# A rebuilt opening for a routed two-layer kernel: dense slots, four gathers at once, a joint first norm

## The reference

```
x = x + tanh(g_xattn) * xattn(layernorm(x), token_ids, ctx)
x = x + tanh(g_ffn)   * ffn(layernorm(x))
```

## Time and profile before

| | us |
|---|---|
| median of three runs | 538.0 (536.31 to 539.51) |
| the profiled execution | 538.59 |
| its span, first to last instruction | 536.8 |
| TensorE matmul busy | 465.1 (87%) |
| VectorE busy | 351.8 (66%) |
| ScalarE busy | 253.8 (47%) |
| GpSimd busy | 242.3 (45%) |
| mean granted clock of TensorE | 0.974 of full speed |

### The profile page before, as it was taken

One profiled execution on the slowest core, in us unless ns is written; L12 is line 12 of the kernel. 1 busy time (PEld: TensorE's weight loads), 2 busy tenths in 40 slices (PEclk: granted clock), 3 DMA queues, 4 the chain that ended last, 5 costly groups with the idle time before them and its releaser, 6 DMA issues.

```text
span 536.8 us, 9049 instructions
## 1 busy us (share of the span) xinstructions
PE 465.1 (87%) x2774; PEld 403.7 (75%) x2775; DVE 351.8 (66%) x766; ACT 253.8 (47%) x381; POOL 242.3 (45%) x266
## 2 busy tenths in 40 slices
PE   1058999999993699999998999999999999999970
PEld 1035777777882488778887999999999998988960
DVE  6657999999986643689485676666665555555510
ACT  4323444444543444621243666666665556555520
POOL 0545455555532000021463546566666656663542
PEclk9999999999998599999999999999999999999995
DMA  8407343444541644022473798888888889876553
GB/s 283 141 20 274 109 154 122 156 157 154 173 135 57 195 140 194 0 79 80 156 249 124 224 321 244 247 254 239 240 234 232 217 234 253 241 246 159 101 65 49
DMA packets 28665, 93.32 MB, mean 174 GB/s; under 512 B 4448, under 2 KB 4448, under 8 KB 28128
## 3 DMA queue, kind: packets, MB, share of 16 engines
q1 hardware_dynamic: 15696, 57.87, 32.9%
q0 software_dynamic: 12944, 35.14, 25.7%
HBM read 71.49 MB, written 23.07 MB: 176 GB/s over the span
## 4 chain that ended last, share of the span: by engine, by line
PE 31%; DMA 29%; DVE 14%; issue 10%; POOL 9%; ACT 3%; POOLq 1%; SPq 0%; DVEq 0%
DMA out<-ys,cur 24%; PE psG L995 17%; PE psY L995 11%; POOL out L424 5%; POOL cur L346 4%; PE psT L1000 3%; DMA front<-in_x,cur 2%; DMA raw<-in_ctx_t 2%; DVE nwt L767 1%; DMA xh<-xh_sb,cur 1%; DVE stats L737 1%; DVE nwt L775 1%; DVE nwt L768 1%; DVE slot L791 1%; DVE gu L717 1%
## 5 line engine op out<-in xcount | busy, mean ns | idle before, releaser
L995 PE MATMUL psY<-arena 128*128 (+1 forms) x372 | 91.6, 397 | 3.2 <-DVE arena L728 3.2
L346 POOL COPY cur<-idx 128x1 int32 (+1 forms) x121 | 50.3, 416 | 93.9 <-DMA out<-ys,cur 30.9
L995 PE MATMUL psG<-bl,slot 128*128 128x256 f32 (+1 forms) x648 | 89.1, 298 | 2.1 <-DVE bl L946 2.1
L995 PEld LDWEIGHTS psG<-bl,slot 128*128 128x128 f32 x648 | 84.1, 193 | 6.8 <-DVE bl L946 2.5
L995 PEld LDWEIGHTS psY<-arena 128*128 128x128 f32 x372 | 67.9, 188 | 17.1 <-issue 3.9
L424 POOL DMA_INDIRECT out<-ys,cur x32 | 64.8, 2025 | 26.6 <-POOL cur L346 18.2
L791 DVE TENSOR_TENSOR slot<-raw,slot 128x1536 fp32r<-128x1536 f32 x27 | 48.4, 1802 | 38.5 <-ACT slot L488 28.5
L995 PEld LDWEIGHTS psG<-bl,arena 128*128 128x128 f32 x576 | 70.0, 192 | 2.2 <-DVE bl L946 1.3
L995 PE MATMUL psG<-bl,arena 128*128 128x256 f32 x576 | 70.6, 283 | 0.9 <-DVE bl L946 0.9
L403 POOL TENSOR_TENSOR xh_sb<-ys,xb 128x512 f32<-128x512 f32 x16 | 21.4, 1339 | 94.8 <-ACT ys L529 84.9
L415 POOL DMA_INDIRECT ht<-xh,cur x32 | 51.0, 1595 | 25.5 <-POOL cur L346 16.5
(11 more groups left out here) (169 smaller groups left out, 621.9 us busy)
## 6 DMA issues: line engine op xcount, KB each, us to landing
raw<-in_w SPq DMA_DIRECT2D x51, 768.0 KB
ht<-xh SPq DMA_DIRECT2D x16, 256.0 KB, 2.8
xb<-xh SPq DMA_DIRECT2D x16, 256.0 KB, 3.0
out<-xh_sb SPq DMA_DIRECT2D x16, 256.0 KB, 2.0
raw<-in_ctx_t SPq DMA_DIRECT2D x2, 1024.0 KB, 8.1
ht<-in_ctx_t SPq DMA_DIRECT2D x1, 1024.0 KB, 11.1
xh_sb<-in_ctx_t SPq DMA_DIRECT2D x1, 1024.0 KB, 13.9
out<-log_sb SPq DMA_DIRECT2D x2, 256.0 KB, 12.9
```

Of the source, the lines that this page charges most:

```text
L346: pool.tensor_copy(cur[:, n:n + 1], table[:, bass.ds(q, 1), col]).then_inc(done, 1)
L995: ins = pe.matmul(ps, left[a], right[b], start=n == 0 and m == 0, stop=n == total - 1 and m == 2)
```

## The change

It touches the opening and the first layer's use of GpSimd. Nothing of the second layer is changed.

- Slots are dense: tokens sorted by expert get positions 0 to 2047 without padding, and slot p of tile `(position >> 7) + expert` is row `position & 127`. A tile in which two experts meet becomes two tiles with the same rows divided between them; there are 19 as before. The rounding of counts goes, a third small matmul (a lower triangle) and some additions come.
- The one-hot matrix is made from 2-byte operands (`digits`, which ScalarE copies from the constants, and `lo_digit`) and lies in `big_all` instead of `front`.
- VectorE makes all four low parts of the context: 0, 1 and 2 behind the index table, 3 at the end of step -1.
- The constants are loaded in two pieces; the loads of the ids and gates are issued by ScalarE.
- GpSimd sends the gathers of tiles 0 to 3 at once (2 and 3 into `ys`, which the first layer doesn't use), without `cur`: each indirect DMA names its column of `idx1`. Its steps are all unrolled.
- Tiles 1 and 2 are normed together in step -1; step 0 has no norm.

```diff
+            def rows_of(t, col):
+                return bass.IndirectOffsetOnAxis(ap=idx1[:, t, col:col + 1], axis=0)
+            def gather_xa(t):
+                if 4 <= t < 6:
+                    pool.wait_ge(h_ready, t - 3)
+                elif t >= 6:
+                    pool.wait_ge(h_ready, t - 1)
+                buf = ys[:, t % 2, :] if t in (2, 3) else xa[:, t % 2, :]
+                pool.indirect_dma_start(buf, None, x, rows_of(t, 0)).then_inc(xa_here[t if t < 4 else t % 2], 16)
+            def gather_xb(t):
+                if t >= 2:
+                    pool.wait_ge(x1_ready, t - 1)
+                pool.indirect_dma_start(xb[:, t % 2, :], None, x, rows_of(t, 0)).then_inc(xb_here[t % 2], 16)
...
+            for t in range(4):
+                gather_xa(t)
+            gather_xb(0)
+            gather_xb(1)
+            gather_xa(4)
+            gather_xa(5)
+            for t in range(2, LAST):
+                if t < NT:
+                    gather_xb(t)
+                if t + 4 < NT:
+                    gather_xa(t + 4)
+                scatter(t - 2)
```

On VectorE, the index table (`S` and `SI` are columns of scratch):

```diff
+            link(dve.tensor_tensor(S(3), S(1), S(2), ALU.add))
+            link(dve.tensor_tensor(S(3), S(3), S(7), ALU.add))
             dve.wait_ge(in_const, 16)
-            link(dve.tensor_tensor_scan(S(8, E1), cst[:, C_KEEP:C_KEEP + E1 * NJ], S(4, E1), 0.0, ALU.mult, ALU.add))
+            link(dve.tensor_tensor_scan(run, ones[:, 0:E1 * NJ], S(4, E1), 0.0, ALU.mult, ALU.add))
...
             dve.wait_ge(r1_pre, 1)
-            link(dve.tensor_scalar(cnt_i[:, 0, :], psY[0][:, E1:2 * E1], float(P - 1), None, ALU.add))
-            link(dve.tensor_scalar(cnt_i[:, 1, :], cnt_i[:, 0, :], -P, None, ALU.bitwise_and))
-            link(dve.tensor_copy(S(13)[:, 0:E1], cnt_i[:, 1, :]))
-            link(dve.tensor_tensor_scan(S(14)[:, 0:E1], ones[:, 0:E1], S(13)[:, 0:E1], 0.0, ALU.mult, ALU.add))
-            link(dve.tensor_tensor(S(15)[:, 0:E1], S(14)[:, 0:E1], S(13)[:, 0:E1], ALU.subtract))
-            link(dve.tensor_tensor(S(16)[:, 0:E1], S(15)[:, 0:E1], psY[0][:, 0:E1], ALU.add))
...
-            link(dve.tensor_copy(S(26, 2), SI(1, 2)))
-            dve.tensor_tensor(onehot[0], along(iota, NJ), over(S(26), P), ALU.is_equal)
+            dve.tensor_tensor(onehot1, along(digits[:, :], NJ), over(lo_digit[:, :], P), ALU.is_equal)
...
-            low_ctx(0)
             dve.wait_ge(r1_src, 1)
...
+            low_ctx(0)
             low_ctx(1)
+            low_ctx(2)
```

On VectorE, the step; `pair` is step -1, and its last Newton operation raises `norm_ready` by 2:

```diff
-                one, two = have(known, 2), have(known, -2)
+                one, two = have(known, 2) and known != 0, have(known, -2)
...
+                pair = known == FIRST + 1
+                cs = slice(0 if one else 1, 2 if two or pair else 1)
...
+                if pair:
+                    xa_landed(dve, 0, 0, 0)
+                    i = dve.bn_stats(stats[:, 1, :], xa_of(0, 0, 0))
...
+                        if pair and m == 0:
+                            low_h()
...
+                if pair:
+                    low_ctx(3)
```

On TensorE:

```diff
-            pe.matmul(psY[0][:, 0:E1], tri, S12(small)[:, 0:E1], start=True, stop=True)
+            pe.matmul(psY[0][:, 0:E1], tri, S12(small)[:, 1:E1 + 1], start=True, stop=False)
+            pe.matmul(psY[0][:, 0:E1], low_tri, S12(small)[:, 0:E1], start=False, stop=True)
```

More of the change, by code:

```diff
@@ L47 @@
 PAD = TOK
-C_ID, C_TRI, C_ONE, C_IOTA = 0, P, 2 * P, 3 * P
+C_TRI, C_LOW, C_ONE, C_IOTA = 0, P, 2 * P, 3 * P
 C_TOKP, C_TOKJ = 4 * P, 4 * P + NJ
-C_KEEP = C_TOKJ + NJ
+C_ID = C_TOKJ + NJ
+C_KEEP = C_ID + P
 C_EM = C_KEEP + E2 * NJ
@@ L194, in gated_layer @@
         xa_idx, xb_idx, xh_idx = sem("xa_idx"), sem("xb_idx"), sem("xh_idx")
-        xa_here = [sem(f"xa_here{n}") for n in range(2)]
+        xa_here = [sem(f"xa_here{n}") for n in range(4)]
         xb_here = [sem(f"xb_here{n}") for n in range(2)]
@@ L237, in gated_layer, with xa_of, xa_landed @@
         FIRST, LOOP0, LOOP1, LAST = -2, 5, 17, NT + 2
+        def xa_of(t, par, known):
+            return ys[:, par, :] if known in (0, 1) else xa[:, par, :]
+        def xa_landed(eng, t, par, known):
+            if known is not None and known < 2:
+                eng.wait_ge(xa_here[known + 2], 16)
+            else:
+                eng.wait_ge(xa_here[par], landed(t, par))
         def stage1(eng, step):
@@ L349, in index @@
                 return bass.IndirectOffsetOnAxis(ap=cur[:, n:n + 1], axis=0)
-            pool.wait_ge(r1_idx, 1)
[L352 to L364, removed]
@@ L479, in step @@
                         act.wait_ge(hT_ps, t + 1)
-                    norm(h[:, par, :], xa[:, par, :], 0, h_ready)
+                    norm(h[:, par, :], xa_of(t, par, known), 1 if known == 0 else 0, h_ready)
                 if have(known, -2):
@@ L738, in step @@
                 k = t + 2
-                if not (one or two):
-                    dve.tensor_copy(stats[:, 0, 0:1], cst[:, 0:1]).then_inc(norm_ready, 1)
-                else:
+                if one or two:
                     i.then_inc(stats_done, 1)
@@ L748, in step @@
                         i = dve.bn_aggr(mv[:, 0, :], stats[:, 0, :])
-                    if two:
+                    if two or pair:
                         i = dve.bn_aggr(mv[:, 1, :], stats[:, 1, :])
@@ L783, in NORMS @@
             def NORMS(k, known):
-                return k + 1
+                return (1, 2, None, 3)[k] if known is not None and known < 2 else k
             stage1(dve, step)
```

93 lines of the change are left out of this document (43 added, 50 removed).

## The result

| | before | changed |
|---|---|---|
| median of four runs each, us | 537.15 (535.44 to 539.51) | 530.6 (527.3 to 531.39) |
| the profiled execution | 538.59 | 530.69 |
| its span | 536.8 | 528.9 |

The ratio is 0.9877 [0.9834, 0.992]: the change gains 1.2%. On another chip later, six runs of the changed kernel gave 529.44 beside 538.06, a ratio of 0.9848 [0.9812, 0.9884]. (The 538.06 is the median of eleven runs of the kernel before, one of them a slow one of 1216.4 us, which the ratio leaves out.) Forecast were 527.4 and a range of 523.2 to 532.5. The direction was right, and 2.7 us of the 10.6 forecast are missing in the span of the two profiled executions, which differ by 7.9; the two medians differ by 6.6. The 2.7 us are not one loss but several terms of both signs.

A forecast was written before the change was run, and what follows sets the result against it. The prediction saw 33.4 us before tile 0's product with TensorE almost idle, two slow tiles, then TensorE nearly always busy. Gains 6.0 + 2.9 + 1.5 + 0 + 0.2 = 10.6 us took 538.0 to 527.4, range 523.2 to 532.5.

The forecast's parts named there:

- tile 0's product: Opening: tile 0's product starts at 27.45 us instead of 33.44, a gain of 6.0.
- tiles 1 to 2, 2 to 3: After the opening: TensorE sets the pace, so 9.26 and 7.90 us become 6.4 each, gaining 2.9 and 1.5.
- 12 tiles: First layer's loop: scatter still holds a short VectorE operation; gain taken as 0, though 3.3 us if freed.
- rival C: Opening: gathers starve behind VectorE's unbroken subtractions, so 3.4 of the 6.0 us go; 530.8 us, chance 0.22.
- The prediction's own sign for the whole: Wrong altogether if the first layer's end does not move by as much as tile 3's product.
- The index table: Opening: table complete at 13.7 us instead of 16.95, from operations removed, added and moved.
- the dearer end of its range: One-hot compare in the opening: stays at 2.29 us; the other end was about 1.2, 1.1 us less.
- From the table to tile 0: Opening: three subtractions end at 20.45 us, gathers land in time, tile 0's norm starts at 23.85, its product at 27.45.
- I leave the first product its 4.95 us: Tile 0's product on TensorE: its length stays as before, so no gain or loss from it.
- rival B: Loop: scatter moves out of VectorE's way or tiles fall into TensorE's pace, 3.3 us more; 524.1 us, chance 0.22.
- the last scatter loses its copy, -0.2: End of the first layer: the last scatter no longer copies its index, a gain of 0.2 us.
- rival D: First layer: unrolled GpSimd sets the pace because its code must be fetched; 541.5 us at 7.5 per tile, chance 0.04.

The follow-up runs named there:

- E1: Changed kernel with the ids loaded by SP ahead of the constants; tile 0's product at 27.37 us instead of 28.48, span 528.3.
- E2: Changed kernel with the gates' load moved from ScalarE to SP ahead of the constants; ids used at 2.75 us instead of 3.68, span 531.0.
- E8: Changed kernel with the subtractions for experts 2 and 3 back on GpSimd behind its four gathers; tile 0's product at 36.83 us, span 536.5.
- E3: Changed kernel with the last tile's scatter writing no row; scatter 2.07 us instead of 3.33, span 526.4.
- E6: Changed kernel with tiles 1 and 2 normed one by one; tile 1 to 2 takes 8.87 us instead of 6.44, span 530.2.
- V2: Changed kernel plus early ids by SP, later residual gather, halved last scatter, expert 2's subtraction at the end of step -1; median 526.5 us, ratio 0.9788.
- E4: Changed kernel with the residual's gather waiting for the step's statistics; 12 tiles take 77.61 us instead of 78.66, span 527.0.
- E5: Changed kernel with index copies back before every indirect DMA; 12 tiles take 78.58 us, tile 0's product at 31.10, span 531.5.
- V1: Changed kernel plus ids by SP, later residual gather and last tile scattered in halves; median 529.19 us, ratio to before 0.9826.
- E7: Changed kernel with the subtraction for expert 0 back ahead of the table's last operations; tile 0's product at 29.87 us, span 528.6.

## Why the prediction was right in direction and 2.7 us too good

Point by point, gains in us:

| step | forecast | measured | |
|---|---|---|---|
| tile 0's product | 6.0 | 4.96 | ids 1.1 late, not priced |
| tile 0 to 1 (7.05 before) | 0 | -0.53 | 7.58: the first product takes 5.48, not 4.95, all at the slow pace |
| tiles 1 to 2, 2 to 3 | 2.9, 1.5 | 2.82, 1.47 | |
| tiles 3 to 5 | 0 | -0.11 | 0.05 per tile, unexplained |
| 12 tiles | 0 | 1.05 | |
| last tiles, scatter | 0.2 | -1.26 | full last tile |
| second layer | 0 | -0.5 | cause not shown; single executions spread by 4.6 |
| sum | 10.6 | 7.9 | |

The sum stands inside its range partly by luck: the loop's gain of 1.05, for which 0 was put, hides most of the 1.26 that the last scatter costs. That the median, 530.6, falls beside rival C's 530.8 is chance too, as C's mechanism did not occur. The prediction's own sign for the whole held roughly: the layer's end moved by 8.4 us, tile 3's product by 8.7.

**The index table.** The sum on it was right but for a term that it doesn't have. "The loads of the ids and gates are issued by ScalarE" stands in the change, and the prediction never says what that costs, while it does say that the constants now come first. E1 and E2 show the term: 1.1 us. The compare stayed at 2.29 with 2-byte operands (L688), and the dearer end of its range was the right one. By the Trainium skill, "VectorE: DVE Perf Modes", section "What auto-detection actually checks", the faster rate wants a step of 1 or -1 in every 16-bit tensor. The digit's step is 0, and the row now agrees: 2.29 us, no faster than before.

**From the table to tile 0.** From tile 0's statistics to its product it was 7.0 forecast and 6.98 measured. The gathers' instructions were forecast at 16.8, 19.0, 21.2 and 22.9; less the 1.1 of the ids they ended 17.1, 19.1, 21.3 and 22.6. Rival C, starving gathers, fell by these rows. The first gather's instruction ended at 18.21, in the middle of the second subtraction, as the earlier trace rows had it, and its rows were there in time for the statistics. The Trainium skill, "SBUF — State Buffer", section "Who interferes with whom", infers that a `tensor_tensor` leaves descriptor work alone; the 2.93, 1.72 and 1.86 beside `tensor_tensor` and 0.95 beyond it don't agree. The subtraction moved off GpSimd was sized by its stall of 2.57, which was right for what went; E8 shows that undone in the new order it would cost 8.35.

**Tiles 0 to 2.** Right in all distances but the first. The step that failed there is "I leave the first product its 4.95 us". It takes 5.48 in the changed kernel and 3.0 for the same twelve matmuls later. How long it takes follows from how much of it lies before the clock's first record, as shown at E3: 2.94 us of it give a product of 4.38 us (E3), 3.33 give 4.55 (E6), 4.18 give 4.95 (the kernel before, V2), 4.88 give 5.27 (the kernel before, again), and in the other nine runs, where the record starts 5.27 to 5.98 us after the product does, nearly all of it is at the slow pace and takes 5.44 to 5.49. So the 0.53 us are paid at the pace of half clock (1.2 GHz). What decides when the clock rises isn't shown.

**The loop.** My step said that the gap of 0.77 to 0.87 in front of each DMA would stay and so the scatter would hold L763 or L764 in each step. Both halves failed: with the index named in place the gap is 0.30, and the scatter went clear, as in rival B. But B's 3.3 didn't come either. In part this is the residual's gather, which slid into the scatter's place: E4 shows another 1.05 behind the gain of 1.05. The 2.1 together are still 1.2 short of B's 3.3, since without any stall a tile takes 6.42 to 6.48 and not the 6.39 that B went by. That the gap alone is not what decides is E5's answer. GpSimd is busy 33.84 of the 78.66, so rival D never came near.

**The end of the layer.** The step "the last scatter loses its copy, -0.2" looked at the instruction and not at its data. The chain of before showed 2.09 for a scatter of nothing; I took it for the price of a scatter. E3 shows the term. The copy's own gain came: from ScalarE's last operation to the scatter it is 0.77 now and 1.08 before. But it was lost just ahead of it, where VectorE now pauses for 0.47 us before it aggregates the last tile's statistics (159.38 to 159.85), as the scatter of the tile before ends (159.78). That this scatter causes the pause isn't tested.

**The second layer** moved as a whole, less 0.5, which is well within the spread of single executions. In the changed kernel the clock is granted at half (1.2 GHz) from 160.4 for 20.4 us, in the one before from 170.7 for 17.1, both beginning in the 11 to 12 us in which TensorE waits for the last scatter and its reload. E1, E2 and E5 to E8 have 20.4 to 20.5 again, E4, V1 and V2 17.0 to 17.1. E4 has the full last scatter, so the 3.4 us aren't tied to that. Nor are they seen in the time: E7 with 20.5 took 357.5 from "end" on, the kernel before with 17.1 took 358.4. What ends the stretch isn't shown.

## What to carry to other kernels

A small load that a long chain starts from has to be issued ahead of the first large one, whatever queue it is on. Ask of each transfer on the path how many rows it really moves in this input: dense packing can turn a free empty transfer at the end of a stage into a full one. When one engine's schedule shifts, a short VectorE operation may meet another DMA's instruction in place of the old one, so look at the whole period and move the DMA behind the short operations with a wait that costs nothing. And a mean of the granted clock can hide a slow start: compare the spacing of equal matmuls, early and late.

## What the runs showed of the hardware that was not expected

- Two loads issued within 0.01 us of each other, on two queues: the small one (128x16 int32) was usable at 3.63 to 3.78, against 2.38 to 2.59 when issued first and 2.75 when the large one came one issue later.
- Indirect DMAs follow one another on GpSimd in 0.30 us if the index is used in place, and in 0.77 to 0.87 behind an index copy.
- A 0.17 us `tensor_scalar` that meets the last 0.4 us of such an instruction takes up to 0.43 and ends with it, while 2048-element subtractions beside a gather keep their 2.2 to 2.3 us and the gather waits instead.
- A GpSimd subtraction of 2048 elements (4.5 us) holds a one-element VectorE `tensor_tensor` until its end (5.05 and 4.40 for 0.16).
- A scatter of 128 rows took 2.07 us with all rows out of bounds, 2.73 with 2 KB each and 3.33 with 4 KB each.
- The matmuls of the first product run 0.43 us apart, as in a stretch with the clock granted at half, and 0.22 to 0.26 us apart from the clock's first record on, 31.6 to 42.3 us into the span. The profile's views print 1.00 for the time before that record.
